# Waits, adds and routing work moved in a two-layer attention and expert kernel, and the second slot table one expert slot earlier

## What is computed

```python
x = x + attention_a(norm(x))     # 16 heads, latent width 32, rotary, causal
x = x + experts(norm(x))
x = x + attention_b(norm(x))     # 16 heads of 8, causal
x = x + experts(norm(x))         # the same weights
```

## Time and profile before

| | |
|---|---|
| median of 3 runs | 1197.36 us |
| lowest, highest | 1195.26, 1198.99 us |
| the profiled execution | 1191.1 us |
| its span, first to last instruction | 1189.4 us |
| PE busy, share | 1024.3 us, 86% |
| POOL | 758.7 us, 64% |
| DVE | 747.3 us, 63% |
| ACT | 648.2 us, 55% |
| mean granted TensorE clock, share of full speed | 0.908 |
| moved by DMA | 91.10 MB |

### The profile page before, as it was taken

The page is one execution under the profiler, slowest core; times in us unless marked ns, Lnnn a source line. Parts: engine busy times, 40 slices in busy tenths (PEclk is TensorE's granted clock), DMA queues, the critical chain, the costliest instruction groups (busy, mean ns, idle before and its releaser), DMA issues. The chain is left out here.

```text
span 1189.4 us, 29763 instructions
## 1 busy us (share of the span) xinstructions
PE 1024.3 (86%) x11227; PEld 793.5 (67%) x11227; DVE 747.3 (63%) x1845; ACT 648.2 (55%) x1193; POOL 758.7 (64%) x824
## 2 busy tenths in 40 slices
PE   4799999999988987999877899999988878999820
PEld 3566776676765666999874556666655557999820
DVE  5878888888889954622345677777777626322332
ACT  1476777776755543455445667767755424455410
POOL 2788988888876746277663477667534233577765
PEclk9799999999998897999997999999988658999975
DMA  9100011010000023578940000000000024688732
GB/s 263 4 2 20 19 38 37 20 37 16 6 11 2 11 72 93 162 232 251 217 121 1 1 15 24 25 16 23 13 8 4 10 98 133 182 239 222 241 104 68
DMA packets 69805, 91.10 MB, mean 77 GB/s; under 512 B 15074, under 2 KB 49762, under 8 KB 69666
## 3 DMA queue, kind: packets, MB, share of 16 engines
q1 hardware_dynamic: 58226, 68.98, 18.4%
q0 software_dynamic: 9088, 18.63, 7.3%
q10 hardware_dynamic: 2352, 1.58, 0.5%
HBM read 68.45 MB, written 20.71 MB: 75 GB/s over the span
## 5 line engine op out<-in xcount | busy, mean ns | idle before, releaser
L1417 ACT ACTIVATE PT<-PS 128x768 f32<-128x768 f32 x256 | 207.1, 809 | 133.0 <-PE PS L1925 79.2
L608 POOL TENSOR_SCALAR_AFFINE_SELECT PT<-PT 128x512 f32<-128x512 f32 x256 | 179.4, 701 | 144.1 <-ACT PT L1417 143.5
L621 POOL DMA_INDIRECT xg<-normed,source x156 | 148.0, 949 | 94.8 <-DVE source L1101 48.1
L1448 ACT ACTIVATE hid<-PS,b_cols 128x256 f32<-128x256 f32 x312 | 122.5, 475 | 113.3 <-PE PS L1664 110.5
L1983 PE MATMUL PS<-W,hid 128*128 x1248 | 158.9, 283 | 0.1
L1983 PEld LDWEIGHTS PS<-W,hid 128*128 128x128 f32 x1248 | 152.6, 199 | 0.6 <-issue 0.5
L730 POOL DMA_INDIRECT got<-expert_rows,slot_of x128 | 122.7, 959 | 40.2 <-issue 34.4
L1311 DVE TENSOR_TENSOR y_rows<-PS,b_rows 128x256 f32<-128x256 f32 x78 | 33.1, 425 | 149.0 <-PE PS L1983 144.1
L1755 PE MATMUL PS<-PT,v_aug 128*32 128x256 f32 (+1 forms) x2048 | 117.9, 352 | 2.2 <-POOL PT L608 2.1
L1737 PE MATMUL PS<-causal_b,ident_b 128*128 128x256 bf16 x512 | 104.1, 287 | 13.5 <-DVE q_aug L1260 12.9
L1662 PE MATMUL PS<-xg_hi,w_ring 128*128 128x256 f32 x312 | 96.9, 311 | 16.7 <-DVE xg_lo L1167 13.0
(11 more groups left out here) (301 smaller groups left out, 2993.2 us busy)
## 6 DMA issues: line engine op xcount, KB each, us to landing
w_ring<-halves_w SPq DMA_DIRECT2D x78, 512.0 KB
expert_rows<-y_rows SPq DMA_DIRECT2D x78, 128.0 KB, 3.1
normed<-xn SPq DMA_DIRECT2D x16, 256.0 KB, 2.3
xg<-normed,source POOLq DMA_INDIRECT x156
W<-in_L_ffn_w_dram SPq DMA_DIRECT2D x1, 2048.0 KB, 13.8
halves_w<-w_hi SPq DMA_DIRECT2D x8, 256.0 KB, 2.3
halves_w<-W SPq DMA_DIRECT2D x8, 256.0 KB, 2.0
got<-expert_rows,slot_of POOLq DMA_INDIRECT x128, 2.7
```

The source lines that it names most:

```text
L608: nc.gpsimd.affine_select(out=diagonals, in_=diagonals, pattern=[[0, 4], [1, P]], compare_op=ALU.is_ge, fill=0.0, base=0, channel_multipli ...
L621: nc.gpsimd.indirect_dma_start(out=xg[:, i % AHEAD, b_, :], out_offset=None, in_=normed if i >= EARLY else normed[0:NH * P, :], in_offset= ...
L1417: s.activation(PT[:, unit % 2, pair, :, :, :], PS[:, 4:6, 0:3 * P].rearrange("p h (a q) -> p a h q", q=P), ACT.Exp).then_inc(m["exp_done"], 1)
L1448: ins = s.activation(hid[:, r % 2, k, :], h_bank[r % 2][k // 2][:, k % 2 * ROWS:(k % 2 + 1) * ROWS], ACT.Gelu, bias=b1_cols[:, bass.ds(e * ...
```

## The change

Six edits. (1) The wait for the bias moves from ahead of the loop to slot 0, between `route_second(0)` and `finish(0)`. (2) `ADDED_AT` goes from 28 to 30, the last slot no longer takes all that is left, and the 5 adds left over (27 to 31) go with the weights of the second half (`weigh(1)`) into `last_results`: for layer 1 called in attention b's prologue right behind the first step (x_lo), for layer 2 right behind the expert loop. The statistics of chunks 0 and 1 move along, to slots 33 and 36. (3) ACT's normalization of chunk 0 for attention b moves from slot 37 to 36. (4) In attention b, DVE does `route_first` ahead of the late step in units 47 to 63, where it stood last in the unit. (5) In units 56 to 63, where PE has no early step, it runs three products of 128 x 512 into bank 7 whose result nobody reads (`unread`), behind a wait for the last reader of the bank. (6) `TABLE_AT` goes from 5 to 4: PE's 32 table products, and DVE's `late_experts` and `sources`, move from slot 5 to slot 4.

```diff
--- before.py
+++ after.py
@@ -38,10 +38,10 @@
 EARLY = -(-(2 * NH * P - E * (ROWS - 1)) // ROWS)
 FIRST_DONE = 2 * NH * P // ROWS + E - 1
 FIRST_BLOCKS = FIRST_DONE * RB
-ADDED_AT = FIRST_DONE + 5
+ADDED_AT = FIRST_DONE + 7
 ADDS = 3
 RESULTS = 8 * CT
-TABLE_AT = 5
+TABLE_AT = 4
 SPLIT_AT = UNITS
 EPS = 1e-5
 MASKED = -1e30
@@ -295,8 +295,10 @@
 def adds_in(i):
 
     k = ADDS * (i - ADDED_AT)
-    end = RESULTS if i == TILES - 1 else min(k + ADDS, RESULTS)
-    return range(k, end) if i >= ADDED_AT else range(0)
+    return range(k, k + ADDS) if i >= ADDED_AT else range(0)
+
+
+ADDED = ADDS * (TILES - ADDED_AT)
 
 
 def split_at(unit):
@@ -1263,6 +1265,8 @@
                 own.then(v.memset(M[:, :, :], 0.0))
                 for s in plan.prologue:
                     closing(m, w, s, False)
+                    if s is plan.prologue[0]:
+                        last_results("1")
                     if (s.kind, s.g) == ("key", 0):
                         row_max(m, 0, 3 * HD)
                 for unit in range(NCH * UNITS):
@@ -1277,6 +1281,8 @@
                         closing(m, w, plan.early[unit], False)
                     if unit + 1 < NCH * UNITS:
                         row_max(m, unit + 1, 3 * HD)
+                    if unit > plan.ROUTE:
+                        route_first(m, w, moe_sems["2"], plan, unit)
                     if plan.late[unit]:
                         closing(m, w, plan.late[unit], False)
                     if c == 0:
@@ -1295,7 +1301,8 @@
                             tile_statistics(c - 1, range(CT), 1)
                         if u == 7:
                             end_statistics(m, 1)
-                    route_first(m, w, moe_sems["2"], plan, unit)
+                    if unit <= plan.ROUTE:
+                        route_first(m, w, moe_sems["2"], plan, unit)
                 close(m, w, plan, "b")
 
             def experts(n):
@@ -1334,17 +1341,18 @@
                         lane_hots(1, 1)
                     elif i == 4:
                         hots(1, 1, m)
-                    elif i == TABLE_AT:
+                    if i == TABLE_AT:
                         late_experts()
                         dve.wait_ge(m["table_ready"], 1)
                         sources(m, y_bank[(TABLE_AT + 1) % 2][:, 0:BLOCKS])
 
-                dve.wait_ge(m["bias_ready"], 16)
                 for i in range(TILES):
                     if i + 2 < TILES:
                         split_rows(m, i + 2)
                     if i <= TABLE_AT:
                         route_second(i)
+                    if i == 0:
+                        dve.wait_ge(m["bias_ready"], 16)
                     finish(i)
                     if i == TABLE_AT + 1:
                         weigh(0, m)
@@ -1355,8 +1363,12 @@
                     if n == "1" and i == ADDED_AT + 6:
                         dve.wait_ge(m["got_used"], 4 * CT)
                         statistics(att_sems["b"], 1, 1)
-                dve.wait_ge(m["got_used"], RESULTS)
-                weigh(1, m)
+
+            def last_results(n):
+
+                add_results(n, range(ADDED, RESULTS))
+                dve.wait_ge(moe_sems[n]["got_used"], RESULTS)
+                weigh(1, moe_sems[n])
 
             def add_results(n, rows):
 
@@ -1383,6 +1395,7 @@
             experts("1")
             attention_b()
             experts("2")
+            last_results("2")
             for c in range(RESULTS // (2 * CT), NCH):
                 add_expert_rows("2", c, range(2 * CT))
 
@@ -1596,7 +1609,7 @@
                         gelu(m, i + 1)
                     if i == TILES - 2:
                         gap_exponent(n, 1)
-                    if n == "1" and i == TILES - 2:
+                    if n == "1" and i == TILES - 3:
                         normal("b", 0, 1, 0)
 
 
@@ -1932,6 +1945,12 @@
                     b_, g = divmod(u, G)
                     weighted(m, unit, g, b_, g // 2 * S)
 
+                def unread(last):
+
+
+                    pe.wait_ge(m["freed_act" if last.by_act else "freed_dve"], last.freed)
+                    product(bank[7], w["hi"][0][:, 0:P], w["lo"][0][:, 0:P], x_hi[:, 1, :], x_lo[:, 1, :])
+
                 causal(range(4))
                 for s in plan.prologue:
                     step(s)
@@ -1946,6 +1965,8 @@
                         causal((2, 3))
                     if plan.early[unit]:
                         step(plan.early[unit])
+                    elif unit >= end - UNITS:
+                        unread(next(s for u in range(unit - 1, 0, -1) for s in (plan.extra[u], plan.late[u], plan.early[u]) if s))
                     if unit + 1 < end:
                         pe.wait_ge(m["aug_ready"], unit + 1)
                         causal((0, 1))
```

## The result

The changed kernel takes 1183.17 us, the median of 4 runs (1181.49 to 1189.55), against 1198.17 us for the kernel before in the same sessions (4 runs, 1195.26 to 1203.04). The ratio is 0.9876, with a 95% interval of 0.9832 to 0.9920: some 15 us faster. The forecast was 1184.4 us. The time was right; the parts of its sum were not all right, and most of what follows is about that.

The account below looks back on a forecast made before the run. PE (TensorE) was taken to bound the kernel, together with late row gathers of POOL. Layer 1's 3.4, attention b's 3.8 and layer 2's 5.8 sum to 13.0 us, subtracted from the median 1197.36: 1184.4 us, range 1177 to 1194.

Parts of the forecast that it names:

- Bias and table: Start of both expert layers: bias wait and slot table moved; 0.3 us lost in layer 1, 0.7 won in layer 2.
- finds the bias landed: Layer 2: the moved wait, before the first y_rows at 996.45, finds the bias landed (it had by 995.67).
- Adds in layer 2: Layer 2, slots 28 to 38: results added from slot 30; slot 38 ends at 1133.9, not 1139.03; 5.1 us won.
- No add waits. At PE's pace: Layer 2, slots 28 to 36: results land in time, no add waits, and slots run at 3.41 us each.
- rival 2: Expert layers: weight ring becomes the bound; 2.5 us less in layer 2, 1 in layer 1: 1188 us; chance 0.10.
- Adds in layer 1: End of layer 1: adds from slot 30; first scores of attention b at 625.2 instead of 628.57; 3.4 us won.
- PE itself would win 9.6 us here: Layer 1, adds from slot 30: PE wins 9.6 us (619.52 against 609.9), but attention b starts on DVE and POOL.
- Rival 3: End of layer 1: adds, statistics, POOL, last gathers form one chain; slow landings; 4.9 us slower, 1202.3 us; chance 0.05.
- Last chunk of attention b: Attention b, units 48 to 63 and first tiles: 2.1 us lost, 2.5, 1.5 and 1.9 won, sum 3.8.
- rival 1: Last chunk of attention b: the added products stay at 1.2 GHz; total 4.3 us won, 1193.1 us; chance 0.17.
- upper end of layer 1: Unknown term of layer 1: between 6.4 us won and 2 lost, against the 3.4 us forecast.
- (c): Before layer 2's tile 0: source list and weight loads move ahead of the last turn step; 1.9 us won.

Follow-up runs that it names:

- e4: Changed kernel with route_first behind the late step again in every unit, unread products kept; 1187.17 us, ratio 0.9915 to the kernel before.
- e5: Changed kernel with the adds of layer 1 alone from slot 28 again, as before the change; 1182.27 us, ratio 0.9874 to the kernel before.
- e7: Changed kernel with the second slot table in slot 5 and layer 1's adds as before the change; 1179.64 us, ratio 0.9849 to the kernel before.
- e9: Changed kernel with distinct rows gathered for empty places and the second slot table in slot 5; 1174.88 us, ratio 0.9830 to the kernel before.
- a0_again: Changed kernel run and profiled again with no edit; 1183.07 us, ratio 0.9878 to the kernel before.
- e2: Changed kernel with adds from slot 28, weights and normalization as before the change, in both layers; 1184.73 us, ratio 0.9889 to the kernel before.
- e11: Changed kernel with the second slot table in slot 5 and adds as before the change in both layers; 1179.87 us, ratio 0.9865 to the kernel before.
- e1: Changed kernel with the second slot table back in slot 5; 1173.55 us (1176.42 with two long runs), ratio 0.9807 to the kernel before.
- e8: Changed kernel in which empty places gather the row of their partition's number instead of row 0; 1176.48 us, ratio 0.9852 to the kernel before.
- e10: Changed kernel with distinct rows for empty places, table in slot 5, adds, statistics and weights as before in both layers; 1173.05 us, ratio 0.9813.

## Why the prediction was right, and where it was not

**Bias and table (0.3 lost in layer 1, 0.7 won in layer 2): right as a sum.** B is 32.2 before and 32.5 in the mean of the changed kernel's two profiles, H 33.6 and 32.35. The wait for block_hot was forecast at 2.9 and 2.7 us and came at 2.63 and 2.59. Behind it, in layer 2, the granted clock was 0.50 from 1014 to 1019 and 0.79 from 1019 to 1023, where the kernel before had 1.00 and 0.57. The first gather of tile 9 was forecast 4.1 and 5.3 us earlier and came 3.9 and 4.6 to 4.9 earlier, counted from the rank products. But the sum hides two large terms of opposite sign, some 6 us won by the bias and some 5 lost by the table, and a reader of the prediction would not guess that the kernel is better without edit (6). One step was wrong without effect on the sum: "finds the bias landed". It landed 1.23 us late in the changed kernel's layer 2 (1.3 to 1.4 in e4, e5, e7 and e9) and in time in a0_again. And the price was read one way only: I booked the early gathers to both edits, though the table brought just 0.6 to 1 us of them.

**Adds in layer 2 (5.1 us): the right stretch, the wrong cause.** J + K is 41.2 before, 37.6 and 39.9 changed, so 1.3 to 3.6 us were won. But e2 and e11, with adds from slot 28, have 36.7 and 37.5. In e2 the stall was gone because the results came earlier against the slots; that it shortened by this in the changed kernel too is likely and not shown by itself. The step that failed is "No add waits. At PE's pace": the adds no longer wait, but PE then waits for w_ring, 2.05 us in a0_again. This was rival 2, priced at 2.5 us for layer 2 and held at 0.10; as a mechanism it happened in layer 1 of every profile with repeated rows, and in layer 2 of a0_again and e1.

**Adds in layer 1 (3.4 us): wrong.** D + E + F is 54.7 before, 56.0 and 56.9 changed: 1.3 to 2.2 us lost. Two steps failed. "PE itself would win 9.6 us here" rested on the 5.46 us in the earlier trace rows. Beside it stood a wait of PE of 3.51 us for weights, in the same slot, which I had not read; it stays when the adds leave, and came out at 5.35 us over two slots in the first profile. So slot 33 came late, and the first root with it: POOL waited 18.71 us for var_eps, and not 10. And the last part, F, was forecast at 15.3 us (609.9 to 625.2) behind a last slot 9.6 us earlier; it is 12.0 and 11.7, behind a last slot that D + E bring only 1.7 and 0.5 us earlier (44.0 and 45.2 against 45.7). The three kernels with distinct rows show where the 3.4 us lay. In e8 and e9, where nothing stalls, slot 27 to the first scores takes 50.4 and 50.5 us, near the 51.3 of the prediction (573.9 to 625.2), and POOL waits 8.8 and 7.1 us for var_eps. But e10, with the adds of before, takes 50.1. So the forecast gain was the price of the stall, not of the place of the adds: it comes when the stall goes, wherever the adds stand. x_lo did come ahead of the adds, as foreseen, but the first query stands behind all five and their landings. Rival 3 (this chain) came true in its sign only, by the late start: the gathers at the end of the chain landed in 2.5 us (median of the 16 from 613 to 636).

**Last chunk of attention b (3.8 us): right in its mechanisms, too small.** G is 7.0 us shorter than in the one profile of before. In a0_again the granted clock is 0.83 from 914 to 924 and 1.00 from there to 954, and the mean clock is higher with the added products (0.917 to 0.933 against 0.909 to 0.917), so rival 1 is refuted. Units 56 to 63 fell from 42.2 to 35.2 and 35.8 us (37.9 in three of the experiments), where I had put 4.0 us for it. Of the 2.1 us lost by the order, e4 shows 0.77 and 0.76 in units 48 and 49. The 1.9 us at the tiles came out at 1.90 and 1.96 in the changed kernel's profiles (4.62 to 2.72 and 2.66), which is partly luck: over the twelve profiles with the new order it is 0.8 to 2.2, and against e4 3.3. What I missed is that the order may shorten the last chunk too: with it and without any added product the chunk took 38.0 us and not 42.2, and the gaps at aug_ready and the clock differ between the two. Each of these is one profile, so this is not shown.

The 6.4 us that the forecast has as the upper end of layer 1, and the 3 us that its range takes from it, are a term that no run shows. What the runs show: the gathers at the end of layer 1 landed in 2.5 us in the changed kernel, those beside streaming weights in 3.8 us in e8 (570 to 580), and the 9 to 11 us from issue to landing of the first results went away with the repeated rows of the empty places. The layer 1 term came out negative with quick landings all the same. At the first tiles the gain of (c) is there: against e4, where the weight loads start 0.45 us ahead of the gathers and not 7.0, PE waits 3.3 us less.

**Sum.** Predicted 13.0, measured 15. By the stages that the change touches (B, D to H, J), the changed kernel's two profiles are 8.7 us shorter in the mean than that of before, and I had 13. 7.0 of the 8.7 are G. What makes up the rest to the medians' 15 no profile shows: the one of before was a short execution (44 of 50 later ones took 1187.9 to 1207.0 us), and A alone spreads over 11 us. Nor do the experiments close the sum: undone one at a time, adds, products, order and bias cost 1.7, 1.9, 4.1 and 3.8 us and the table gives back 6.7 to 9.5, which leaves 2 to 5 us of the 15, each number with an interval of several us. That part stays open. So the time was met by terms that erred in both directions: adds 8.5 forecast and about 1.7 found in e2, attention b 3.8 forecast and 1.9 and 4.1 found for its two parts one by one, bias and table 0.4 and about 0.9. That they met at the median is luck in good part.

## What to carry to other kernels

Before a wait is removed, read what every other engine does in the same microseconds: here PE's wait of 3.51 us for weights stood beside DVE's 5.46 us for results, and when the adds left slot 28 it was still there, 5.35 us over two slots. Where many waits gather in one stretch, ask the DMA view for the time of one packet there; here one clamp, which sent every empty place to the same row (0.73 us a packet instead of 0.10), was behind both DVE's wait for the first results and PE's for the weights. And see whether the bottleneck engine then stands at a dependency that ends in the same slot: here the table moved one slot earlier bought the difference of the ends (0.6 to 1 us), not the slot, and paid with PE's wait (2.6 us a layer; some 5 us in all over both layers). Two edits booked as one small sum should be tested one by one: here the better kernel had only one of them.
